# Attention and a routed mixture of experts on one core: expert weights split once into high and low parts, expert products as three fp32r products

## The reference, cut to what matters

```python
xn = layernorm(x)                                   # x: 2 x 1024 x 512
# attention: 16 heads of 32, causal, rotary q and k
qkv = xn @ w_attn + b_attn
o = softmax(mask(q @ k.T)) * 512 ** -0.5 @ v
attn = o @ w_proj + b_proj
# mixture of experts on the same xn: 8 experts, 2 of them for each of the 2048 rows
probs = softmax(xn @ gate_w.T); topw, sel = top_k(probs, 2); topw /= topw.sum()
g, u = split(xn @ w1[e].T)                          # w1[e]: 704 x 512, two halves of I = 352
y_e = (silu(g) * u) @ w2[e].T                       # w2[e]: 512 x 352
out = x + attn + sum_e combine[e] * y_e
```

## Time and profile before

| | us |
|---|---|
| median of 3 runs | 932.34 (927.4 to 936.08) |
| the profiled execution | 932.23 |
| its span in the trace | 930.4 |
| TensorE busy in the span | 850.4 (91%) |
| VectorE, ACT, GpSimd busy | 368.2, 290.8, 272.6 |
| bytes moved by DMA | 143.20 MB, 154 GB/s over the span |

### The profile page before, as it was taken

One profiled execution on the slowest core, in us unless ns is written; L12 is line 12 of the kernel. 1 busy time (PEld: TensorE's weight loads), 2 busy tenths in 40 slices (PEclk: granted clock), 3 DMA queues, 4 the chain that ended last, 5 costly groups with the idle time before them and its releaser, 6 DMA issues. The chain is left out here.

```text
span 930.4 us, 12421 instructions
## 1 busy us (share of the span) xinstructions
PE 850.4 (91%) x3661; PEld 524.0 (56%) x3662; DVE 368.2 (40%) x1137; ACT 290.8 (31%) x622; POOL 272.6 (29%) x352
## 2 busy tenths in 40 slices
PE   3889999389999999999999989999999999999990
PEld 3668988255555555555555434566666656666650
DVE  5983452574666666666674021111111111111110
ACT  3221221004545555556555400112221211222210
POOL 4781000305233242332331610033332323333330
PEclk9899999758999999999999998999999999999995
DMA  9386596876357666576730137536445455433326
GB/s 318 143 264 206 197 314 203 252 171 228 97 156 186 187 191 153 178 199 173 189 83 14 42 112 258 169 69 156 107 107 158 73 156 147 81 68 64 57 29 201
DMA packets 76716, 143.20 MB, mean 154 GB/s; under 512 B 12928, under 2 KB 26752, under 8 KB 76608
## 3 DMA queue, kind: packets, MB, share of 16 engines
q1 hardware_dynamic: 38192, 65.68, 22.7%
q10 hardware_dynamic: 29056, 58.28, 22.1%
q0 software_dynamic: 9424, 18.69, 10.8%
HBM read 81.21 MB, written 61.15 MB: 153 GB/s over the span
## 5 line engine op out<-in xcount | busy, mean ns | idle before, releaser
L1286 ACT ACTIVATE probs<-scores_t 128x512 f32<-128x512 f32 (+3 forms) x384 | 163.7, 492 | 143.8 <-PE scores_t L1413 130.2
L883 PE MATMUL gu<-w,rows_t 128*128 x624 | 197.4, 459 | 1.1 <-DVE o_t L849 1.1
L1390 PE MATMUL maxima<-k_stack,q_stack 96*128 96x512 f32 (+3 forms) x384 | 141.2, 388 | 14.7 <-DMA q_stack<-qk_hi 8.7
L883 PEld LDWEIGHTS gu<-w,rows_t 128*128 128x128 f32 x624 | 115.2, 190 | 69.7 <-issue 19.7
L1433 PE MATMUL o_acc<-probs,v_ones 128*64 128x512 f32 (+3 forms) x768 | 147.9, 507 | 0.0
L1413 PE MATMUL scores_t<-q_stack,k_stack 98*128 98x512 f32 (+3 forms) x384 | 138.0, 385 | 5.6 <-DMA q_stack<-row_lo 3.5
L1316 DVE CUSTOM_DVE_ANT_0 masked_scores<-maxima,mask_m 128x128 f32<-128x128 f32 (+3 forms) x256 | 121.3, 485 | 23.5 <-PE maxima L1390 19.3
L1320 DVE TENSOR_REDUCE mx<-maxima 128x1 f32<-128x512 f32 x128 | 88.2, 689 | 86.4 <-PE maxima L1390 86.3
L1413 PEld LDWEIGHTS scores_t<-q_stack,k_stack 98*128 98x128 f32 x384 | 73.1, 193 | 67.9 <-issue 42.2
L901 PE MATMUL down<-w,hidden_t 128*128 (+1 forms) x234 | 107.0, 592 | 0.8 <-DVE hidden_t L857 0.8
L1390 PEld LDWEIGHTS maxima<-k_stack,q_stack 96*128 96x128 f32 x384 | 76.8, 202 | 35.6 <-DVE mx L1320 9.9
(11 more groups left out here) (148 smaller groups left out, 930.7 us busy)
## 6 DMA issues: line engine op xcount, KB each, us to landing
w<-in_w_t SPq DMA_DIRECT2D x8, 1408.0 KB, 6.5
routed<-blank_row ACTq DMA_DIRECT2D x20, 514.0 KB, 6.9
rows<-routed ACTq DMA_DIRECT2D x39, 256.0 KB
qk_hi<-st_hi SPq DMA_DIRECT2D x32, 256.0 KB, 4.8
qk_lo<-st_lo SPq DMA_DIRECT2D x32, 256.0 KB, 6.1
q_stack<-qk_hi ACTq DMA_DIRECT2D x32, 256.0 KB, 4.1
k_stack<-qk_hi ACTq DMA_DIRECT2D x26, 256.0 KB, 5.2
v_all<-o_t SPq DMA_DIRECT2D x4, 1536.0 KB, 5.7
```

Source lines behind the costliest of these rows:

```text
L883: last = nc.tensor.matmul(gu[r][j][:, 0:I], rows_t[r][:, k * P:(k + 1) * P], w1[:, bass.ds(e, 1), k, j * I:(j + 1) * I].rearrange("p o n - ...
L1286: nc.scalar.activation(probs[:, k % PR, h, 0:w], scores_t[e % RING][:, 0:w], ACT.Exp).then_inc(exp_done, 1)
L1390: nc.tensor.matmul(mb[at % RING][:, 0:w], q_st[i][0:3 * HD, h, t * P:(t + 1) * P], k_st[i][0:3 * HD, h, c * CH:c * CH + w], start=True, st ...
```

## The change

In attention, beside the rounds, the weights of all 8 experts are read in 88 pieces (`PIECES`; 11 for each expert: 8 of 128 x 352 and 3 of 128 or 96 x 512), one in each segment from the last segment of round 0 to segment 2 of round 15. SyncE loads a piece, ACT copies its high part to an fp32r tile after the exponentials of the segment (VectorE does so for the last 6 pieces), VectorE subtracts to get the low part, and SyncE stores both parts in memory and loads the piece after next. There are two buffers of each kind. In `experts`, `load_weights(e)` reads both parts (four DMAs) into two ring buffers; rows and hidden values are split as well (high part by ACT, low part by VectorE, where a plain copy stood); each up product becomes 3 times 4 products of 352 columns for a half and the down product 3 times 3 of 512. The third part of the hidden values is padded from 96 to 128 columns. Routing counts at least one tile for each expert. In the diff below, lines that only rename, allocate or add semaphores are left out.

```diff
+UP_COLS = DK * 2 * I
+W_COLS = UP_COLS + len(I_TILES) * D
+PIECES_E = DK * 2 + len(I_TILES)
+PIECES = E * PIECES_E
...
+        link(V.tensor_scalar(tiles[:], tiles[:], 1.0, None, ALU.max))
...
-        w1 = m.sbuf("w1", [P, RING_E, DK, 2 * I], F32)
-        w2 = m.sbuf("w2", [P, RING_E, len(I_TILES), D], F32)
+        w_hi = m.sbuf("we_hi", [P, RING_E, W_COLS], F32R)
+        w_lo = m.sbuf("we_lo", [P, RING_E, W_COLS], F32R)
...
             def load_weights(e):
                 at = e % RING_E
-                sp.dma_start(w1[:, at], w1_t[e].rearrange("(k p) n -> p k n", p=P)).then_inc(weights_in[e], 16)
-                sp.dma_start(w2[:, at, 0:2, :], w2_t[e, 0:2 * P, :].rearrange("(k p) n -> p k n", p=P)).then_inc(weights_in[e], 16)
-                sp.dma_start(w2[0:I - 2 * P, at, 2, :], w2_t[e, 2 * P:I, :]).then_inc(weights_in[e], 16)
+                last = W_COLS - D
+                for tile, source in ((w_hi, scratch["w_hi"]), (w_lo, scratch["w_lo"])):
+                    sp.dma_start(as_f32(tile[:, at, 0:last]), source[e, :, 0:last]).then_inc(weights_in[e], 16)
+                    sp.dma_start(as_f32(tile[0:I - 2 * P, at, last:W_COLS]), source[e, 0:I - 2 * P, last:W_COLS]).then_inc(weights_in[e], 16)
             def announce(e):
-                sp.wait_ge(weights_in[e], 3 * 16)
+                sp.wait_ge(weights_in[e], 4 * 16)
...
+            for r in range(2):
+                nc.gpsimd.memset(hidden[r][:, I:], 0.0).then_inc(hidden_padded, 1)
...
-                nc.scalar.copy(rows_t[r][:], turn_ps[:]).then_inc(turned_read, 1)
+                nc.scalar.copy(rows_hi[r][:], turn_ps[:]).then_inc(rows_hi_done, 1)
+            def hidden_high(i, r):
+                act.wait_ge(hid_turned, i + 1)
+                if not early(i):
+                    act.wait_ge(y_full, i - 1)
+                nc.scalar.copy(hidden_hi[r][:], hid_ps[:, 0:len(I_TILES) * P].rearrange("p (k t) -> p k t", t=P)).then_inc(hid_hi_done, 1)
...
                 nc.scalar.activation(gated[:], gu[r][0][:, 0:I], ACT.Silu).then_inc(silu_done, 1)
+                if past(i, 1):
+                    hidden_high(i - 1, 1 - r)
...
-            def hidden_to_sbuf(i, r):
-                dve.wait_ge(hid_turned, i + 1)
+            def rows_low(i, r):
+                dve.wait_ge(rows_hi_done, i + 1)
+                if not early(i):
+                    dve.wait_ge(gu_full, 2 * (i - 1))
+                nc.vector.tensor_tensor(rows_lo[r][:], turn_ps[:], as_f32(rows_hi[r][:]), ALU.subtract).then_inc(turned_read, 1)
+            def hidden_low(i, r):
                 if not early(i):
                     dve.wait_ge(y_full, i - 1)
-                nc.vector.tensor_copy(hidden_t[r][:, 0:2, :], hid_ps[:, 0:2 * P].rearrange("p (k t) -> p k t", t=P))
-                nc.vector.tensor_copy(hidden_t[r][0:I - 2 * P, 2, :], hid_ps[0:I - 2 * P, 2 * P:3 * P]).then_inc(hid_read, 1)
+                dve.wait_ge(hid_hi_done, i + 1)
+                nc.vector.tensor_tensor(hidden_lo[r][:], hid_ps[:, 0:len(I_TILES) * P].rearrange("p (k t) -> p k t", t=P),
+                                        as_f32(hidden_hi[r][:]), ALU.subtract).then_inc(hid_read, 1)
             def tile(i, r, half):
-                if not (isinstance(i, int) and i == 0):
-                    hidden_to_sbuf(i - 1, 1 - r)
+                if past(i, 1):
+                    hidden_low(i - 1, 1 - r)
+                if not (isinstance(i, int) and i == SLOT_TILES - 1):
+                    rows_low(i + 1, 1 - r)
                 dve.wait_ge(silu_done, i + 1)
                 dve.wait_ge(gu_full, i * 2 + 2)
                 if not early(i):
                     dve.wait_ge(hid_turned, i - 1)
-                nc.vector.tensor_tensor(hidden[r][:], gu[r][1][:, 0:I], gated[:], ALU.mult).then_inc(hidden_done, 1)
+                nc.vector.tensor_tensor(hidden[r][:, 0:I], gu[r][1][:, 0:I], gated[:], ALU.mult).then_inc(hidden_done, 1)
...
+            def weights(tile, slot, at, n, part=P):
+                return tile[0:part, bass.ds(slot, 1), at:at + n].rearrange("p o n -> p (o n)")
+            def up(i, r, slot, j):
+                out = gu[r][j][:, 0:I]
                 for k in range(DK):
-                    last = nc.tensor.matmul(gu[r][j][:, 0:I], rows_t[r][:, k * P:(k + 1) * P],
-                                            w1[:, bass.ds(e, 1), k, j * I:(j + 1) * I].rearrange("p o n -> p (o n)"),
-                                            start=(k == 0), stop=(k == DK - 1))
+                    hi, lo = (t[r][:, k * P:(k + 1) * P] for t in (rows_hi, rows_lo))
+                    at = (k * 2 + j) * I
+                    nc.tensor.matmul(out, hi, weights(w_hi, slot, at, I), start=(k == 0), stop=False)
+                    nc.tensor.matmul(out, hi, weights(w_lo, slot, at, I), start=False, stop=False)
+                    last = nc.tensor.matmul(out, lo, weights(w_hi, slot, at, I), start=False, stop=(k == DK - 1))
                 last.then_inc(gu_full, 1)
...
-                for k, (at, n) in enumerate(I_TILES):
-                    last = nc.tensor.transpose(hid_ps[0:n, k * P:(k + 1) * P], hidden[r][:, at:at + n], ident[:])
+                if isinstance(i, int) and i == 0:
+                    pe.wait_ge(hidden_padded, 2)
+                for k in range(len(I_TILES)):
...
+            def down_product(i, r, slot):
                 pe.wait_ge(hid_read, i + 1)
                 if not early(i):
                     pe.wait_ge(y_read, i)
-                for k, (at, n) in enumerate(I_TILES):
-                    last = nc.tensor.matmul(down[r][:], hidden_t[r][0:n, k, :],
-                                            w2[0:n, bass.ds(e, 1), k, :].rearrange("p o n -> p (o n)"),
-                                            start=(k == 0), stop=(k == len(I_TILES) - 1))
+                for k, (_, n) in enumerate(I_TILES):
+                    hi, lo = hidden_hi[r][0:n, k, :], hidden_lo[r][0:n, k, :]
+                    at = UP_COLS + k * D
+                    nc.tensor.matmul(down[r][:], hi, weights(w_hi, slot, at, D, n), start=(k == 0), stop=False)
+                    nc.tensor.matmul(down[r][:], hi, weights(w_lo, slot, at, D, n), start=False, stop=False)
+                    last = nc.tensor.matmul(down[r][:], lo, weights(w_hi, slot, at, D, n), start=False, stop=(k == len(I_TILES) - 1))
                 last.then_inc(y_full, 1)
...
+        def piece_of(p):
+            e, q = divmod(p, PIECES_E)
+            if q < DK * 2:
+                k, j = divmod(q, 2)
+                return e, q * I, P, I, w1_t[e, k * P:(k + 1) * P, j * I:(j + 1) * I]
+            at, rows = I_TILES[q - DK * 2]
+            return e, UP_COLS + (q - DK * 2) * D, rows, D, w2_t[e, at:at + rows, :]
+        def high_part(engine, copy, p):
+            _, _, rows, cols, _ = piece_of(p)
+            engine.wait_ge(piece_in[p % 2], 16 * (p // 2 + 1))
+            if p >= 2:
+                engine.wait_ge(piece_out[p % 2], 32 * (p // 2))
+            copy(piece_hi[p % 2][0:rows, 0:cols], w_piece[p % 2][0:rows, 0:cols]).then_inc(piece_hi_done, 1)
...
+            def load_piece(p):
+                _, _, part, cols, source = piece_of(p)
+                sp.dma_start(w_piece[p % 2][0:part, 0:cols], source).then_inc(piece_in[p % 2], 16)
+            def store_piece(n, segment):
+                p = n * NB + segment - (NB - 1)
+                if not 0 <= p < PIECES:
+                    return
+                e, at, part, cols, _ = piece_of(p)
+                sp.wait_ge(piece_lo_done, p + 1)
+                for to, tile in (("w_hi", piece_hi), ("w_lo", piece_lo)):
+                    sp.dma_start(scratch[to][e, 0:part, at:at + cols], as_f32(tile[p % 2][0:part, 0:cols])).then_inc(piece_out[p % 2], 16)
+                if p + 2 < PIECES:
+                    load_piece(p + 2)
...
+                store_piece(n, 0)
+                store_piece(n, 1)
                 sort_out(n, 0)
+                store_piece(n, 2)
                 if n + 1 < ROUNDS:
                     rows(n + 1)
+                if n == 0:
+                    load_piece(0)
+                    load_piece(1)
+                store_piece(n, 3)
+                store_piece(n, 4)
                 if n % PAIRS == 0 and n:
                     store_shares(n // PAIRS - 1)
+                store_piece(n, 5)
...
+                    if n and k % BATCH == BATCH - 1 and (n - 1) * NB + k // BATCH < HIGH_ON_DVE:
+                        high_part(act, nc.scalar.copy, (n - 1) * NB + k // BATCH)
...
+            def low_part(p):
+                _, _, part, cols, _ = piece_of(p)
+                if p >= HIGH_ON_DVE:
+                    high_part(dve, nc.vector.tensor_copy, p)
+                dve.wait_ge(piece_hi_done, p + 1)
+                if p >= 2:
+                    dve.wait_ge(piece_out[p % 2], 32 * (p // 2))
+                nc.vector.tensor_tensor(piece_lo[p % 2][0:part, 0:cols], w_piece[p % 2][0:part, 0:cols],
```

(3 more changed lines are left out.)

56 lines of the change are left out of this document (37 added, 19 removed).

## The result

| | before | after |
|---|---|---|
| median | 934.2 us (927.4 to 1116.7, 4 runs) | 1012.4 us (1010.0 to 1016.4, 4 runs) |
| span of the profiled execution | 930.4 | 1008.1 |
| mean granted clock | 0.957 | 0.911 |

What follows compares the result with a forecast made beforehand. The prediction took TensorE to bound attention rounds and expert tiles, with the loop through the tag close behind in the tiles. It summed 932.2 + 34 (pieces) - 12 (loop) - 2 (first tiles) to 952 us, range 910 to 985.

Steps and rivals of the forecast that it cites:

- Pieces in the rounds: Attention: the pieces' DMA work lengthens 12 rounds from 19.74 to 22.6 us, +34 us, bounds nothing to +55.
- Products: Expert tiles: cheaper fp32r products cut TensorE's tile by 1.34 to 6.74 us, 52 us over 39 tiles if TensorE stays the bound.
- The loop: Expert stage: y, add and tag load bound the tiles; 33 intervals of 6.9 and 5 of 13 make 293 us, 12 less.
- ACT and VectorE arithmetic at nothing: Attention rounds: at most 0.62 us of ACT and 0.85 of VectorE per segment, covered by TensorE's value products, counted as nothing.
- The first two tiles, -2: Start of the expert stage: the two tiles ahead of the first y save 2 us more.
- R3: Rival, everything at its dear end: attention +65, experts +4, about 1000 us; chance 0.10.
- R1: Rival, pieces hidden in idle DMA time: attention costs 0 to 8, experts give 14 to 30, 916 us likeliest; chance 0.22.
- R4: Rival, the loop isn't a bound: tiles become 6.74 us everywhere, 880 us with hidden pieces; chance 0.04.

Runs made afterwards that it cites:

- e1: After with `store_piece(n, 0)` issued ahead of `spread_shares` and `load_totals` on SyncE; 986.4 us, ratio 1.059.
- e6: e1's order plus a third buffer for loaded pieces, so a load is issued one segment earlier; 987.6 us, ratio 1.059.
- e7: e6 with the next tag's load moved ahead of the add; 979.4 us, ratio 1.050.
- e15: e7, all 88 pieces, with the `share_rows` loads issued at the end of the even round; 980.1 us, ratio 1.051.
- e11: e7 with experts 0 to 2 split in place during the output projection, so only 55 pieces go through attention; 969.9 us, ratio 1.035.
- e14: e12 with the `share_rows` loads issued at the end of the even round; 942.2 us, ratio 1.010.
- e17: e4 with the next tag loaded early, low part of the weights left out; 902.6 us, ratio 0.968.
- e16: The kernel before with only the next tag's load moved ahead of GpSimd's wait for y; 932.5 us, ratio 1.000.
- e3: After with GpSimd loading the next tag before it waits for y; 999.4 us, ratio 1.067.
- e9: e4 plus all 88 copies and subtractions, on two pieces loaded once, no other piece moved; 919.5 us, ratio 0.984.
- e4: After's expert half alone: no pieces in attention, both ring buffers loaded from unsplit weights, same bytes and products; 916.9 us, ratio 0.980.
- e12: e11 with the same 55 pieces moved to segments 4, 5 and 0; 952.8 us, ratio 1.020.
- e8: e6 without the low stores; the experts load the high part twice; 971.6 us, ratio 1.044.
- e10: e8 with three buffers for the high parts too and one for the unstored low part; 975.5 us, ratio 1.043.

## Why the prediction was wrong in size

*The step that failed* is in "Pieces in the rounds": "So 24.4 / 1.08 = 22.6 us, 2.9 more than 19.74". The numerator was right: 13.0 us of work that was there and 11.4 for the pieces; measured, 24.3 in all and 10.9 for the pieces. The divisor was not. It assumes that the engines can be kept full through the whole round. They reached 0.86 in after, and 0.92 to 0.95 in the other orders of six pieces (e1, e6, e7, e15). A piece's load, copy, subtraction and store wait for each other with two buffers, and SyncE issues them between waits for other things. 24.3 / 0.86 is 28.2; the added round was 8.5 us and not 2.9. By parts: 88 us in attention, 76 of them in rounds 3 to 11 and 12 in the others, for +34.

*The deeper fault* is that a sum of DMA work is only a lower bound, and no price. With half the pieces in a round the work fits into 20 us, and the round was still 22 to 25 (e11 to e14). What costs is that one transfer with a deadline comes late, and then twice: the stop, and the clock behind it. There are three such transfers, one behind the other: the load of a piece behind `load_totals` or `share_rows` (moved in e1); `share_rows` itself, with the masks behind (moved in e14); `row_lo`, which no run moved, so that its share rests on the waits alone. My text named the first path ("ACT waits in its own queue for a piece to have landed") and the last ("at the deadline already, so 0 to 0.7 us a round"), but gave neither a price in the sum (the last, 0 to 10 us, at the upper end only). `share_rows` it didn't name, though its wait, 5 times and 44 us in the rounds of before, was in the trace.

*The clock* had no term in my sum; 2.9 us of a round's 8.5 are it. In the trace of before the rounds run at 1.00 throughout, but one place outside them showed a price that I hadn't looked at: ahead of the output projection TensorE stops for 2.63 us, and for the four us after 558.08 its clock is 0.50. The Trainium skill has the rule, "TensorE: Matmul & The Clock Gate", section "HAM oscillation — how this bites in real kernels": a wait for DMA that puts the array back on its lower clock charges its cost anew in each repeat of the loop. By that rule a stop of 5 us in a round would cost more than 5; the trace agrees, with 5.6 us of stops and 2.9 of slower work.

*Products.* Half an up product takes 1.94 us in after (757.39 to 759.33), as forecast; the down product 2.19 (755.20 to 757.39) for 2.09. With the transposes at 0.68 that is 6.75. Over many tiles TensorE comes to 7.0 (e17, where in the stretches without a load every second interval is 6.7 and the others 7.35), with gaps of 0.2 to 0.3 us ahead of some down products. I had 6.74.

*The loop.* Right: 289.9 us for 293. The short intervals are 7.03 for 6.9, those with a load 11.6 for 13: 11.35, 11.57, 11.83, 11.83 and 11.23. The Trainium skill's rule on the engines going round the queues ("DMA: Bandwidth & Descriptors", section "Queues, rings and completion order"), which I had set beside my 13, gave 10.9 and was the nearer. The trace agrees in part. From the list of DMA issues of after around the first such interval (KB each, us from issue to landing):

```profile
we_lo<-w_low_all SPq DMA_DIRECT2D x1, 1920.0 KB, 13.5
...
tag<-routed POOLq DMA_DIRECT2D x1, 1.0 KB, 9.1
```

Both were issued within 0.02 us of each other (720.94 and 720.96), and the tag landed 4.4 us ahead of the weights: it didn't wait for the whole load. But its 9.1 us are twice the 4.4 to 5.2 that it takes in intervals without a load. My reading of before was off in one detail that the sum didn't use: behind each load there were two intervals of 6.75 to 7.16 us and a third of 7.4 to 7.8, and not three or four of 6.8 to 7.1.

That the loop, through the tag, bounds the tiles is one reason for a gain of 15 us and not 51: the tag's place is worth nothing to the old products (e16), and 8 to 14 us to the new (e3, e17). It isn't the only one. Even in e17 the 38 intervals are only 32 us shorter than before; TensorE's 7.0 for 6.74 takes 10 us of the rest, and intervals of up to 10.9 us at the weight loads are still there.

*ACT and VectorE arithmetic at nothing.* Right: 2.6 us over all rounds (e9), which is within noise of nothing.

*The first two tiles, -2.* Wrong, +5. At the start ACT's issues of `acc<-o_t` held its queue for 30 us (652.20 to 682.3, seven of the eight), while the DMA engines moved the split weights of experts 0 to 2 at a share of 0.99 to 1.06. The high copy of the first rows stands behind them. TensorE waited 7.95 us, and its first half of an up product took 3.68 us at 0.50 of the clock. I had given these loads the output projection as cover, without asking what shares the engines with them. But their bytes alone aren't the cause: e4 loads as many, at a share of 1.05 to 1.07, and reaches its first y 2.5 us sooner than before does; there the `acc<-o_t` transfers land after 10.2 us (median), in after after 15.6. What differs is that after loads them in four DMAs from the stored parts and e4 in six from the unsplit weights. No run separates this, and it stays open.

*The rivals.* R3, "everything at its dear end", was nearest, but at about 1000 still short, since its rounds stood on the same kind of divisor. R1 was to decide from 8.4 us of DMA work or less for a round's pieces; they were 10.9. It would have fallen below that too: in e11 they were 19.8 - 13.4 = 6.4 us a round and weren't hidden. R4 fell at the tag; e17 shows that even without pieces and with the tag early it is 903 and not 880.

Open is how much of the last row, e14, is `row_lo` alone, and why `row_lo`, 8 KB issued 0.6 us after VectorE has made it, lands after 1.8 us in one round and after 6.4 in another (e14), beyond that the engines are full then. Open too is why the clock falls after one stop and not after another of the same length.

## What to carry to other kernels

A free third of the DMA engines isn't room for a third more traffic: look for the loads with a deadline in each full stretch, who waits behind them in order, and price the added traffic by how late these come. A stop of TensorE of a few us in a loop has to be priced with the slow clock behind it: half as much again in after, as much again in e11 and e14. And when an engine becomes faster, see first what was hidden just below it (here the tag's place in GpSimd's queue): that edit was free, and took the expert half from -17 us (e4) to -28 (e17).

## What the runs showed of the hardware

- The stops shown in after (5.2 us), e12 (4.0) and e11 (2.9) had a stretch at 0.50 to 0.54 behind them. In e12 and e11 the DMA share in it fell to 0.20 and 0.01: the slow work came when nothing was waited for any more.
- Not every stop brings the low clock, and its length doesn't decide. In e14 a stop of 1.65 us had 0.50 behind it and one of 1.87 us had 1.00. The stop ahead of the output projection is the same in all runs (2.63 or 2.64 us): in the four us behind it the clock was 0.50 to 0.64 in twelve of the traces (before and after among them) and 1.00 in six (e4, e6, e8, e10, e15, e17).
- Six copies a round on ACT and six subtractions on VectorE, put between work that already filled 57 and 64% of these engines, made the round 0.1 us longer (19.95 in e9, 19.81 in e4).
- In stretches with a DMA share of 1.01 to 1.06 the engines moved 215 and 218 GB/s in e11, 219 and 289 in e12, and 328 and 330 in after: the share tells when they are full, the bytes don't.
- With the engines full from a weight load of 4.33 MB, a load of 1 KB from another queue took 9.1 us to land (after, issued at 720.96), for 4.4 to 5.2 us without such a load, and still landed 4.4 us ahead of the 1920 KB load issued at the same time.
